# Layers zero and one of a four-layer kernel: from a loop over batches to one unrolled pipeline of half-batches

## What is computed

```python
x = x + L0_xattn(ln(x), ctx)     # 16 heads of 16, softmax over 77 keys
x = x + L0_ffn(ln(x))            # routed spline layer with its own layernorm
x = x + L1_xattn(ln(x), ctx)     # 16 query heads, one head of keys and values, causal mask
x = x + L1_ffn(ln(x))            # experts; then layers 2 and 3
```

## Time and profile before

| | |
|---|---|
| time, median of 3 runs | 3204.38 us (3204.13 to 3211.77) |
| the profiled execution | 3211.5 us |
| its span, first to last instruction | 3209.8 us |
| mean granted TensorE clock | 0.883 |
| busy: PE, PEld, DVE, ACT, POOL | 2456.5, 2008.1, 2006.4, 1434.8, 734.8 us |

### The profile page before, as it was taken

The page is one execution under the profiler, slowest core; times in us unless marked ns, Lnnn a source line. Parts: engine busy times, 40 slices in busy tenths (PEclk is TensorE's granted clock), DMA queues, the critical chain, the costliest instruction groups (busy, mean ns, idle before and its releaser), DMA issues. The chain is left out here.

```text
span 3209.8 us, 43539 instructions
## 1 busy us (share of the span) xinstructions
PE 2456.5 (77%) x16502; PEld 2008.1 (63%) x16502; DVE 2006.4 (63%) x4672; ACT 1434.8 (45%) x2407; POOL 734.8 (23%) x639
## 2 busy tenths in 40 slices
PE   0847757657566899999984999999999477677675
PEld 0535525435435788888873999999999345454544
DVE  1776676776674566666653666656565357675856
ACT  0413423433334456565542454444444254555535
POOL 0212212222122234444444000000000452424020
PEclk9868868768777999999996999999999688898887
DMA  8200000000001000010002343434342421111000
GB/s 300 102 0 14 15 0 29 1 1 28 1 1 42 1 20 33 31 40 29 22 18 76 110 145 109 145 109 145 109 145 81 139 64 36 54 36 53 1 14 13
DMA packets 153951, 185.43 MB, mean 58 GB/s; under 512 B 21864, under 2 KB 119429, under 8 KB 153736
## 3 DMA queue, kind: packets, MB, share of 16 engines
q1 hardware_dynamic: 141448, 155.41, 14.8%
q0 software_dynamic: 12288, 27.15, 2.7%
HBM read 117.51 MB, written 71.43 MB: 59 GB/s over the span
## 5 line engine op out<-in xcount | busy, mean ns | idle before, releaser
L2095 POOL DMA_INDIRECT picked<-expert_out,so x128 | 126.4, 988 | 870.8 <-DMA so<-slots 765.4
L204 PE MATMUL SC<-Xhi,Whi 128*128 128x320 f32 x1024 | 319.9, 312 | 7.1 <-DVE Wlo L1888 5.3
L204 PE MATMUL SC<-Xlo,Whi 128*128 128x320 f32 x1024 | 317.0, 310 | 0.0
L204 PE MATMUL SC<-Xhi,Wlo 128*128 128x320 f32 x1024 | 316.9, 309 | 0.0
L1124 POOL TENSOR_TENSOR ff_Hlo<-ff_HF,ff_Hhi 128x512 fp32r<-128x512 f32 x112 | 147.9, 1320 | 423.6 <-ACT ff_Hhi L1257 423.5
L328 POOL TENSOR_TENSOR PR<-PR,rs 128x616 f32<-128x616 f32 x128 | 153.6, 1224 | 325.5 <-DVE rs L294 325.5
L204 PEld LDWEIGHTS SC<-Xhi,Whi 128*128 128x128 f32 x1024 | 193.0, 188 | 7.7 <-DVE Wlo L1888 5.7
L204 PEld LDWEIGHTS SC<-Xlo,Whi 128*128 128x128 f32 x1024 | 193.1, 189 | 0.0
L204 PEld LDWEIGHTS SC<-Xhi,Wlo 128*128 128x128 f32 x1024 | 192.8, 188 | 0.0
L1907 DVE TENSOR_TENSOR Hlo<-HF,Hhi 128x320 fp32r<-128x320 f32 x256 | 125.3, 490 | 104.2 <-ACT Hhi L1865 104.2
L1865 ACT ACTIVATE Hhi<-HF 128x320 fp32r<-128x320 f32 x256 | 120.6, 471 | 154.6 <-DVE HF L1918 154.6
(11 more groups left out here) (454 smaller groups left out, 6950.2 us busy)
## 6 DMA issues: line engine op xcount, KB each, us to landing
expert_in<-zeros SPq DMA_DIRECT2D x4, 5120.0 KB, 31.9
rowsin<-expert_in SPq DMA_DIRECT2D x32, 640.0 KB, 5.8
expert_out<-rowsout SPq DMA_DIRECT2D x32, 640.0 KB, 4.0
Wraw<-L_wg SPq DMA_DIRECT2D x32, 512.0 KB, 7.2
Wraw<-L_wu SPq DMA_DIRECT2D x32, 512.0 KB, 7.0
Wraw<-L_wd SPq DMA_DIRECT2D x32, 512.0 KB, 8.0
Xin<-x SPq DMA_DIRECT2D x10, 512.0 KB, 4.4
x_after_l_attention<-X SPq DMA_DIRECT2D x8, 512.0 KB
```

The source lines that it names most:

```text
L204: last = nc.tensor.matmul(out, lhs[l], rhs[r], start=start and n == 0, stop=stop and n == 2)
L2095: nc.gpsimd.indirect_dma_start(picked[g][:, t, k, :], None, oute[:, :], bass.IndirectOffsetOnAxis(ap=so[g][:, t, k:k + 1], axis=0)).then_i ...
```

## The change

The loop and its two threads are gone. `attention_units` lays out one stream of 128 units over periods of 16 slots. There are 12 periods, h = -1 to 10. In period h the slots 0 to 7 hold the eight units of layer zero of half-batch h (0 to 7), and the slots 8 to 15 those of layer one of half-batch h - 2. So periods 2 to 7 have 16 units, 0, 1, 8 and 9 have eight, and -1 and 10 none. Each slot has one unit, with the same lags of two and three slots. All units share one score bank (`SC[0]`) and one bank for transposes and values (`GP[0]`); the rest of the work shares `mid` (`GP[1]`) and `wide` (`SC[1]`). The rest is spread over the slots by hand, for half-batches p = h + 1, h, c1 = h - 1, c2 = h - 2, c3 = h - 3. On PE it stands between the slot's value products and its transposes, on DVE behind the shift and the sums:

| slot | PE | DVE | ACT | POOL |
|---|---|---|---|---|
| 0 | transposes c1 | | | add spline c2 |
| 1 | | statistics c2 | copy XT c1; replicate context | beta row c1 |
| 2 | signatures, hidden c1; keys (p even) | rstd c2 | root c2 | |
| 3 | | statistics p; values' rest | apply c2; keys; exp and gelu c1 | |
| 4 | components c1; transposes c2 | calibrate c1 | | bias row c2 |
| 5 | | rstd p; components, cluster c1 | root p; copy XT c2 | keys, values of layer one (c2 even) |
| 6 | project out c3; project q c2 | calibrate c1 | exp, tanh c1; apply p | |
| 7 | | add second c3; pick tile c1 | copy q c2 | bias row p |
| 8 | transposes p; one-hot c1 | | | |
| 9 | | | one-hot c1; copy XT p | keys of layer zero (p even) |
| 10 | look-up c1 | | | |
| 11 | | spline c1 | | |
| 12 | project out h | directions, statistics c1 | | |
| 13 | values (p even) | rstd c1; add first, statistics h | root c1 | |
| 14 | project q p | rstd h; values | root h; apply c1 | |
| 15 | | times gamma c1 | apply h; copy q p | values of layer zero (p even) |

Every engine's normal unit work comes in each slot on top. The other moves: the application of a layernorm goes from DVE to ACT (four activations of 128x256 with scale and bias), the replication of the context from DVE to ACT, the building of `Kbd` and `Vbd` from DVE to POOL, the last add of the spline part from DVE to POOL; `calibrate` and `first_max` run on half of the data, twice as often; rstd gets a sixth small operation; the table is looked up in two products (66 and 256 columns) and read in PSUM without a copy; `x` is loaded straight into one of five buffers. The core of the diff:

```diff
+def attention_units():
+    units, at, after = [], {}, {}
+    for h in range(NH + 2):
+        for layer, half in ((0, h), (1, h - 2)):
+            if 0 <= half < NH:
+                for u in range(UNITS):
+                    at[(h + 1) * PERIOD + layer * UNITS + u] = len(units)
+                    units.append((layer, half, u))
...
-        with nc.Fori(0, B) as b:
...
+                    for h in range(-1, NH + 3):
+                        p, c1, c2 = h + 1, h - 1, h - 2
+                        for s in range(PERIOD):
+                            i = (h + 1) * PERIOD + s
+                            now, mixed, valued = (UNIT_AT.get(i - d) for d in (0, LAG, LAG + 1))
...
+                            if now is not None:
+                                exponentials(now)
+                            if valued is not None:
+                                take_ot(valued)
...
+                            if mixed is not None:
+                                take_pt(mixed)
...
+                    def unit_scores(n):
...
+                        if n:
+                            pe.wait_ge(shifted, n)
...
+                    def unit_transposes(n):
+                        pe.wait_ge(pnorm, n + 1)
+                        if n:
+                            pe.wait_ge(pt_ready, n)
+                            pe.wait_ge(ot_ready, n)
...
+                            if now is not None:
+                                unit_scores(now)
+                            if valued is not None:
+                                unit_values(valued)
...
+                            if s == 6 and 0 <= c3 < NH:
+                                if c1 < NH:
+                                    pe.wait_ge(comp_sum, c1 + 1)
+                                project_out(wide, 1, wo1, c3, y1_psum)
+                            if s == 6 and 0 <= c2 < NH:
+                                project_q(wq1, c2, xt_c, q1_psum)
...
+                            if now is not None:
+                                shift(now)
+                            if summed is not None:
+                                sums(summed)
...
+                            if s == 4 and 0 <= c1 < NH:
+                                cluster_gates(c1)
+                            if s == 5 and p < NH:
+                                ln_rstd(p, LN["p"], var_p, sd_p, rstd_p)
```

More of the change, by code:

```diff
@@ L39 @@
 FFN2 = HE // P
+NH = B * G
 ZR = 2
@@ L125, in build @@
         layer_3(**common)
[L128 to L173, removed]
 def four_heads(ap):
@@ L358, in shared_buffers @@
     return w
+NXA = 5
+NPA = LAG + 2
+PERIOD = 2 * UNITS
+def attention_units():
[6 more added lines that the diff above has]
+                    units.append((layer, half, u))
+                after[layer, half] = len(units)
+    return units, at, after
+UNIT, UNIT_AT, AFTER = attention_units()
 def attention_layers(W, late_in, zero_in, xmid, nc, a, sbt, GP, SC, ident, identb, onesf, headof, blockhead, eps, x1, buf, oute, slots, gates, out):
@@ L467, in _ @@
                 sp.wait_ge(zeroed, 1)
-                first = [(ctxT[:, :, 0:CTX], ctxTv[0])] + [(Xin[g][:, :, :], xv[0, g]) for g in range(G)]
+                first = [(ctxT[:, :, 0:CTX], ctxTv[0])] + [(X[g][:, :, :], xv[g]) for g in range(G)]
                 for dst, src in first:
@@ new lines, in keys, with values @@
+                            for k in range(KC):
+                                nc.tensor.matmul(mid[:, V1AT + j * DH:V1AT + (j + 1) * DH], rep(j, k), wv1[:, k, :], start=k == 0, stop=k == KC - 1)
+                        for k in range(KC):
+                            last = nc.tensor.matmul(mid[:, TOK:TOK + D], rep(BLK - 1, k), wv0[:, k, :], start=k == 0, stop=k == KC - 1)
+                        last.then_inc(k_psum, 1)
+                    def values(b):
+                        for j in range(BLK - 1):
+                            for k in range(KC):
+                                last = nc.tensor.matmul(wide[:, j * D:(j + 1) * D], rep(j, k), wv0[:, k, :], start=k == 0, stop=k == KC - 1)
+                        last.then_inc(v_psum, 1)
@@ new lines, in signatures, with compress @@
+                    def signatures(h):
+                        n = NCL + NT
+                        for t in range(TT):
+                            for k in range(KC):
+                                last = nc.tensor.matmul(wide[:, t * n:(t + 1) * n], XT[:, k, t * P:(t + 1) * P], sig[:, k, :], start=k == 0, stop=k == KC - 1)
+                        last.then_inc(sig_psum, 1)
+                    def compress(h):
+                        for k in range(KC):
+                            last = nc.tensor.matmul(wide[0:CH, TOK:2 * TOK], cw1[:, k, :], XT[:, k, :], start=k == 0, stop=k == KC - 1)
+                        last.then_inc(hid_psum, 1)
@@ new lines, in look_up @@
+                    def look_up(h):
+                        pe.wait_ge(oh_ready, h + 1)
+                        for outs, cols, done in ((small, slice(D, D + SMALL), small_psum), (dirs, slice(0, D), dir_psum)):
+                            for t in range(TT):
+                                for n, half in enumerate((table_hi, table_lo)):
+                                    last = nc.tensor.matmul(outs[t], ohT[:, t * P:(t + 1) * P], half[:, cols], start=n == 0, stop=n == 1)
+                            last.then_inc(done, 1)
@@ L935, in late_loads @@
     return loads
-NH = B * G
 SLOTS = 14
```

869 lines of the change are left out of this document (534 added, 335 removed).

## The result

The kernel after the change takes 3235.35 us (median of 5 runs, 3231.67 to 3244.81), the kernel before 3205.97 (3204.13 to 3211.77, 5 runs): a ratio of 1.0094, 95% interval 1.0073 to 1.0116. It is slower, by 29 us; the forecast was slower by 72, at 3276. The direction held, the size was more than twice too large.

What follows compares the result with a forecast made beforehand. No engine is full, so the order of work bounds the kernel. Six periods of 107.7 us are 646; keys add 11, the last saves 6; with 318 for the ends, the stage takes 969, 72 over 896.6: 3276, range 3145 to 3340.

Steps and rivals of the forecast that it cites:

- The bare slot: Attention slot without extra work: a chain from scores to transposes takes 4.2 us for one unit, 5.4 at the lower clock.
- The clock step: Bare slots get the lower clock (1.2 GHz), so 5.4 us each; long PE stretches priced near it, slot 6 half and half.
- The rival with the clock up everywhere: PE at full clock in all slots: period 93 us, stage 854, kernel 3162; chance 0.20.
- the prediction's own signs: In the stage, PE clock near 0.6 would confirm the forecast; over 0.8, or full periods under 96 us, would refute it.
- 2.5 + 4.35 + 3.1: Slot 4 on DVE: bare work 2.5, calibrate 4.35, port waits 3.1; less overlap, 9.5 us.
- The port: DVE operations with two SBUF operands wait for POOL's running operation: 14 us per period, some 10 on the path.
- The table switch: ACT's table load takes 1.28 us and the exponential starts 1.29 after it, with no further drain.
- its rival of 3348: Each ACT table switch holds 1.28 us more, seven a period on the path: 72 us added, 3348; chance 0.05.
- the ends: Periods -1, 0, 1, 8, 9 and the tail, where the pipeline fills and drains: 318 us together.
- the rival without port wait at the low clock: DVE never waits for POOL while PE's clock is low: about 3212; chance 0.09.

Runs made afterwards that it cites:

- a_otfirst: The kernel after, with ACT's copy of the output of the unit before (OT) moved ahead of the roots and the exponential: 3208.0 us, ratio 1.0005.
- a_order: a_otfirst with ACT's PT copy before the gelu in slot 3, and projection and PT copies before the application in slot 15: 3202.04 us, ratio 0.9988.

## Why the prediction was off by more than half

**The bare slot** was right: 4.20 at the upper and 5.4 at the lower level, by the chain scores, maximum, exponential, OT copy, transposes. a_otfirst shows that this chain is the cause: with one link out of it, DVE's 2.5 remains in slot 8.

**The clock step failed**: "I take the lower level (1.2 GHz) in bare slots." The windows show 1.00 in them. Slots 0, 1, 3, 8 and 9 are together 5.1 us shorter than forecast, slots 2, 12 and 14, priced at or near the lower level, 4.3 (8.5 to 5.9, 7.9 to 6.7, 6.4 to 5.9). The step went by PE's busy share, halfway between two rows, and took the nearer to the routing. That share was no guide: slot 1 has PE busy for 2.10 of 4.20 us at 1.00, the same work in period 9 has it for 3.64 of 5.38 at 0.50. Half of the time idle in pauses of 2 us kept the upper level. Nor was a long stretch without PE work what lost it in period 9: just ahead PE was busy for 8.32 of 9.70 us, at 0.94, and the clock fell in slots 8 and 9 of that period, where PE is busy for 1.40 us of each 3.1, and stayed low in the bare slots behind. Windows of after, ahead of period 9 and its slot 9:

```profile
945.00:954.70 9.70, 8.32 (x29) 4.97 (x27) 1.22 (x1) 3.13 (x4) 0.43 (x1) 0.94 0.15 54
...
957.87:961.00 3.13, 1.40 (x4) 0.50 (x4) 2.50 (x5) 0.72 (x1) 0.48 (x1) 0.50 0.00 0
```

Period 0 begins in the same way. Why the bare slots of after keep the level that they are entered with stays open. The rival with the clock up everywhere (854 us for the stage, 93 for a period) is as wrong: slots 4, 10 and 11 are at 0.50 to 0.53, and 930 lies between the two. By the prediction's own signs neither holds, with the clock at 0.74 (near 0.6 forecast, over 0.8 for the rival) and a period of 102 (the rival wanted under 96).

**Three slots were under-priced**, by 4.3 us together, and hide part of that error: that the sign of the forecast was right is partly luck. Slot 10 (7.3 for 6.2) runs wholly at the lower level: with the pause in slot 9 filled it is 4.5. Slot 15 (7.2 for 5.4) has the next scores wait for a projection copy behind an application; the prediction said that ACT's work "hides, except in slot 3", which was wrong here: a_order took 2 to 2.5 us off it. Slot 4 (10.9 for 9.5) is the instructive one. The prediction had 2.5 + 4.35 + 3.1 of DVE and said that the late PT copy doesn't matter there, since DVE bounds that slot. Those terms were sized well: `calibrate` took 7.03 us in slot 4, 2.8 of them waits for POOL, and 4.94 in slot 6, 0.7 of them such waits, so 4.2 by itself. Without `calibrate` the slot did not change: the late copy and PE's queue behind it end last. The sum was near, for the wrong reason.

**The port.** Single waits came as worked out (0.19 to 2.23, 0.42 to 2.52). How much of "some 10" lies on the path was tested for the two bias rows alone, priced at 4.5 us a period. In slot 4 their 2.3 lie beside PE's chain. In slot 7 DVE has no idle time, so that its wait of 2.23 is in the slot's length; without the row the slot is 1.2 to 2.1 shorter, and slot 8 took much of it back. The whole kernel gained 10 us in one order and 4 in the other, 0.5 to 1.2 per half-batch, with the clock of slot 10 moving in both. So 4.5 was too much; the waits of 0.7 behind POOL's normalisation, in DVE-bound slots such as 6, no run took away. By the Trainium skill (GPSIMD Engine Reference, section Specifications) such operations share a port; the trace agrees on the single operation, and what it costs the kernel was in slot 4 a question of the other chain.

**The table switch**: at 471.33 a load of 1.28, and the exponential at 472.63, 1.30 behind it. So the rows bear out the prediction's reading, and its rival of 3348 has nothing in them.

**The account.** Five full periods took 523 us, forecast 5 times 107.7 and 11 for keys, 549.5: 26.5 less. Period -1 took 26.2 for 33, period 0 57.3 for 61, period 1 77.5 for 81, period 7 with the chain behind it 129.5 for 124.7, then 62.6 for 65 and 54 for 55. That is 39 under the forecast's 969, and 930 is what the stage took. The part of the forecast that lay in the ends was off by 12, that of the five periods by 27. Taken by period 4, the slots of the clock step took 47 off these five (9.4 each), the three under-priced slots put 21 back, and keys another 4, since each period with keys is 7.7 us longer and not 5.5. Two slips in the arithmetic weigh nothing: the sixteen slots add to 107.6 and not 107.7, and the rival without port wait at the low clock comes to 3201 by its own terms and not 3212.

**Why the change loses at all**, 29 us at the start and 31 with the order mended. A period is 100 to 102 us, or 110 with keys, against 112.1 for a half-batch before (896.6 over eight), so the five full ones gained 37: 523 for 560. The rest of the stage, 407 us in which the pipeline fills and drains, stands for three half-batches, 336 of before, and loses 71: together the 33.5 of the trace. The order of work gained what it was to gain in the middle, and eight half-batches are too few for its ends. The forecast had these 407 us at 420, so the slow ends were foreseen. This is worked out from the lengths; no run had more half-batches.

## What to carry to other kernels

Look in an in-order queue for a short operation whose input is long there, behind one whose input is late; it took 0.26 us here, two edits of its place were worth 27 and 49 us, while the change of structure cost 29. Before pricing the engine that looks full in a slot, leave its work out: two chains may end together, and only the run shows which is last. Don't take a clock from the busy share; find a stretch with the same pauses and the same past, and where none is, carry both levels through the whole sum. And a pipeline's ends must be set against the number of its periods.

## What was not expected of the hardware

Extra matmuls made the kernel faster: three more value products in a pause of PE kept its clock at 1.00, and the next slot took 4.5 us and not 7.3, with nothing lost in the slot of the pause. A program of equal slots can settle at either level: 4.2 us at 1.00 with PE idle half of the time, or 5.4 at 0.50 with PE busy two thirds of it; what stood ahead of them differed (two slots with PE busy for 1.40 of 3.1 us, where the clock stayed low), and why each keeps its level is not shown. Moving an addition on POOL moved the clock of another slot, from 0.50 to 1.00 in one kernel and from 1.00 to 0.58 in another. And one DVE operation of 0.19 us took 2.23 while POOL ran one addition, but taking two such additions out of DVE's way was worth 4 to 10 us in all.
